# Selective scan: who multiplies the third state of every second group of four

## The reference

```
delta, b, c = split(u @ x_proj_w);  delta = softplus(delta @ dt_proj_w + dt_proj_b)
a = -exp(A_log)
h_t = exp(d_t * a) * h_{t-1} + d_t * b_t * u_t       # for every channel and each of 16 states
y_t = sum over the 16 states of h_t * c_t
y = (y + u * D_param) * silu(x_gate);  out = y @ out_proj_w
```

## Time and profile before

| | us |
|---|---|
| median of 3 runs (lowest, highest) | 2647.35 (2646.22, 2647.95) |
| the profiled execution: its own time | 2645.0 |
| the profiled execution: span of its instructions | 2643.2 |
| the 64 scans: first start, last start | 2329.0, 2521.7 |
| mean granted TensorE clock, share of full speed | 0.984 |

### The profile page before, as it was taken

The page is one execution under the profiler, slowest core; times in us unless marked ns, Lnnn a source line. Parts: engine busy times, 40 slices in busy tenths (PEclk is TensorE's granted clock), DMA queues, the critical chain, the costliest instruction groups (busy, mean ns, idle before and its releaser), DMA issues. The chain is left out here.

```text
span 2643.2 us, 47115 instructions
## 1 busy us (share of the span) xinstructions
PE 2495.8 (94%) x18340; PEld 1932.1 (73%) x18340; DVE 1458.3 (55%) x2420; ACT 1005.5 (38%) x2177; POOL 679.6 (26%) x711
## 2 busy tenths in 40 slices
PE   7889998999999898999999998997999999989999
PEld 4676994666666657967888887894888888467778
DVE  4574225777777743025555556425555555589982
ACT  2252224666666431333222221223222222677731
POOL 2102003001100011013334431203433434057833
PEclk9989998999999999999999999999999999999999
DMA  9353872111110103962212112464121210022210
GB/s 312 123 165 130 299 273 80 45 37 33 33 49 17 54 1 138 327 205 64 72 49 73 61 49 102 153 229 124 61 70 51 73 61 25 27 80 81 86 38 16
DMA packets 98808, 262.25 MB, mean 99 GB/s; under 512 B 19139, under 2 KB 45734, under 8 KB 91062
## 3 DMA queue, kind: packets, MB, share of 16 engines
q1 hardware_dynamic: 86662, 241.84, 27.8%
q0 software_dynamic: 3840, 10.49, 1.3%
q10 hardware_dynamic: 8112, 7.21, 0.8%
HBM read 237.31 MB, written 22.19 MB: 98 GB/s over the span
## 5 line engine op out<-in xcount | busy, mean ns | idle before, releaser
L2685 POOL TENSOR_TENSOR buf<-buf 128x512 f32<-128x512 f32 x128 | 160.0, 1270 | 473.8 <-ACT buf L2831 473.6
L2862 DVE TENSOR_REDUCE buf<-acc 128x256 f32<-128x1024 f32 x128 | 150.8, 1220 | 215.0 <-PE acc L2716 209.8
L2749 PE MATMUL acc<-buf 128*128 128x256 f32 x1024 | 257.0, 384 | 0.0
L2710 PE MATMUL acc<-buf 128*128 128x256 f32 x1024 | 236.6, 384 | 3.2 <-PEq L98 2.3
L2826 ACT COPY buf<-acc 128x256 f32<-128x256 f32 x64 | 23.8, 372 | 532.9 <-PE acc L2731 532.9
L2710 PEld LDWEIGHTS acc<-buf 128*128 128x128 f32 x1024 | 189.4, 190 | 36.6 <-issue 11.8
L2749 PEld LDWEIGHTS acc<-buf 128*128 128x128 f32 x1024 | 180.8, 190 | 33.4 <-issue 15.9
L3227 ACT ACTIVATE buf<-acc,buf 128x512 f32<-128x512 f32 x256 | 172.6, 686 | 75.7 <-DVE buf L3259 75.7
L3259 DVE TENSOR_REDUCE buf<-acc 128x1 f32<-128x512 f32 x256 | 159.0, 684 | 53.6 <-PE acc L3140 53.6
L2875 DVE TENSOR_TENSOR buf<-acc,buf 128x1024 f32<-128x1024 f32 x128 | 150.8, 1220 | 67.8 <-ACT buf L2826 67.8
L3152 PEld LDWEIGHTS acc<-identity,buf 128*128 128x128 f32 x1024 | 114.4, 141 | 82.9 <-issue 78.5
(11 more groups left out here) (506 smaller groups left out, 4768.4 us busy)
## 6 DMA issues: line engine op xcount, KB each, us to landing
buf<-in_L_ffn_W SPq DMA_DIRECT2D x52, 1024.0 KB, 7.0
buf<-in_ctx SPq DMA_DIRECT2D x48, 768.0 KB, 4.5
buf<-in_ctxT SPq DMA_DIRECT2D x64, 512.0 KB, 4.0
buf<-in_L_ffn_w SPq DMA_DIRECT2D x36, 704.0 KB, 5.7
buf<-state_rows SPq DMA_DIRECT2D x32, 512.0 KB, 3.6
buf<-in_ctxT SPq DMA_DIRECT2D x96, 128.0 KB, 4.2
buf<-in_L_ffn_w SPq DMA_DIRECT2D x18, 640.0 KB, 6.4
buf<-in_ctxT SPq DMA_DIRECT2D x32, 256.0 KB, 5.4
```

Source lines behind the costliest of these rows:

```text
L2685: pool.tensor_tensor(quarters[:, 2 * n:2 * n + 2, :], t[:, 4 * n:4 * n + 2, :], t[:, 4 * n + 2:4 * n + 4, :], ALU.add).then_inc(adding, 1)
L2710: pe.matmul(acc_s[:, n, :], ct0[x][:, tile(key_tile(n))], q0[:, b, 4 * y:4 * y + 4, :], start=(n % 2 == 0), stop=False)
L2749: pe.matmul(acc_m[:, 0:ROWS], ctx[x][:, key_tile(n), 0:P], probsT[y][:, n, :], start=(n == 0), stop=(n == KT - 1))
L2862: dve.tensor_reduce(most_of[n][:, :], acc_s[:, 4 * n:4 * n + 4, :].rearrange("p k r -> p r k"), AX.X, ALU.max).then_inc(part_most, 1)
```

## The change

In the quads 1, 3, 5, 7, 9, 11 and 13 (`three_by_pool`), the product R2 goes from DVE to POOL. There POOL's list becomes M0, M1, M2, A0, A1, where M2 multiplies the third state by `crow[1]`; DVE's list becomes s0, s1, s2, s3, R3. The even quads and quad 15 stay as they are. The semaphores count anew: `pool_reads(q)` and `dve_reads(q)` give how many products of each engine lie before quad q. In a changed quad A0 waits for M2 (the instruction just before it on POOL) where it waited for R2. SP's load of `crow[1]` for the quad behind a changed one waits for M2 as well as for R3.

```diff
@@ selective_scan
+            def three_by_pool(q):
+                return q % 2 == 1 and q < QUADS - 1
+
+            def pool_reads(q):
+                return 2 * q + q // 2
+
+            def dve_reads(q):
+                return 2 * q - q // 2
...
                 for m in range(ROUNDS):
+                    before = m // 2 - 1
                     if m >= 2 and m % 2 == 0:
-                        sync.wait_ge(read_by_pool, m)
+                        sync.wait_ge(read_by_pool, pool_reads(before) + 2)
                     elif m >= 2:
-                        sync.wait_ge(read_by_dve, m - 1)
+                        sync.wait_ge(read_by_dve, dve_reads(before + 1))
+                        if three_by_pool(before):
+                            sync.wait_ge(read_by_pool, pool_reads(before) + 3)
...
                 for n in range(UNITS):
                     scan(n)
-                    if n % 4 >= 2:
+                    if n % 4 == 3 or n % 4 == 2 and not three_by_pool(n // 4):
                         read_out(n)
...
                         pool.tensor_tensor(now[:, :], now[:, :], crow[0][:, :], ALU.mult).then_inc(read_by_pool, 1)
+                    if three_by_pool(q):
+                        now = state[(4 * q + 2) % STATES]
+                        pool.wait_ge(rows_in[1], q * 16 + 16)
+                        pool.wait_ge(scanned, 4 * q + 3)
+                        pool.tensor_tensor(now[:, :], now[:, :], crow[1][:, :], ALU.mult).then_inc(read_by_pool, 1)
                     if q < QUADS - 1:
                         for y in range(2):
                             now, other = state[(4 * q + y) % STATES], state[(4 * q + 2 + y) % STATES]
-                            pool.wait_ge(read_by_pool, 2 * q + y + 1)
-                            pool.wait_ge(read_by_dve, 2 * q + y + 1)
+                            pool.wait_ge(read_by_pool, pool_reads(q) + y + 1)
+                            if three_by_pool(q) and y == 0:
+                                pool.wait_ge(read_by_pool, pool_reads(q) + 3)
+                            elif three_by_pool(q):
+                                pool.wait_ge(read_by_dve, dve_reads(q) + 1)
+                            else:
+                                pool.wait_ge(read_by_dve, dve_reads(q) + y + 1)
                             pool.tensor_tensor(now[:, :], now[:, :], other[:, :], ALU.add).then_inc(paired, 1)
```

More of the change, by code:

```diff
@@ L3683, in _ @@
                     if n < UNITS - 2:
-                        pe.wait_ge(read_by_pool, 2 * QUADS - 2 + n % 4 + 1)
+                        pe.wait_ge(read_by_pool, pool_reads(QUADS - 1) + n % 4 + 1)
                     else:
-                        pe.wait_ge(read_by_dve, 2 * QUADS - 2 + n % 4 - 1)
+                        pe.wait_ge(read_by_dve, dve_reads(QUADS - 1) + n % 4 - 1)
                     add_up(n)
```

## The result

The changed kernel takes 2655.32 us (median of 8, 2652.12 to 2659.77) against 2645.72 of the kernel before in the same sessions (median of 8, 2642.35 to 2647.95). The ratio is 1.0035, 95% interval 1.0024 to 1.0046: slower by some 9 us, where 8.7 was forecast. The profiled execution spans 2653.1 us. The 2645.72 is 1.6 under the median of three runs that the prediction was built on (2647.35).

What follows compares the result with a forecast made beforehand. The prediction took one full queue of POOL's and DVE's two-SBUF-input products as the bound. Terms 5.9 + 1.1 + 1.1 + 0.6 for the clock made +8.7, so 2656.1 us; 8-in-10 range 2652.5 to 2659.5.

Steps and rivals of the forecast that it cites:

- What bounds: POOL's products and DVE's two-SBUF-input products exclude each other, forming one full queue of 11.81 us a quad; DVE close second.
- Removing R2: In changed quads, s3 still waits for PE's drive until about 8.1 us; the scan comes forward by 0.1 only.
- Adding M2 and the stretched R3: In changed quads, M2 delays A0, and R3 ends 1.08 behind A0: 13.00 us in place of 11.81, +1.19.
- The wait of A0 for M2: On POOL in a changed quad, A0 waits for the instruction before it: 0.1 us more.
- Quad 9: Despite slack from a PE stall, M2 and A0 stand behind s2 and R3 behind A0 again: +1.1 us.
- Quads 11 and 12: R3 gets in ahead of A0 in quad 11, A0 and A1 slide into quad 12; together about +1.1 us.
- a fall of the clock in quad 12: PE waits about 2.7 us for A0 in quad 12, perhaps then slowing: bounds 0 and 1.4, taken as 0.6.
- The sum: Whole-kernel total: 5.9 for five quads, 1.1, 1.1 and 0.6 for the clock, 8.7 us, giving 2656.1.
- Rival 1: DVE is the bound and gets lighter: changed quads take 10.4 us, -1.4 each, 2637 in all; chance 4%.
- Rival 2: In changed quads R3 goes ahead of A0: +0.6 to +0.8 us each, 2651.6 to 2653; chance 9%.
- Rival 3: No exclusion between M2 or A0 and R3 in changed quads: -1.4 us in all, 2646; chance 2%.
- Rival 4: PE's clock falls in many quads, three to seven more: +4 to +10 us, 2660 to 2666; chance 8%.

Runs made afterwards that it cites:

- e3: Kernel before, with DVE's products R2 and R3 replaced by a maximum with one SBUF input, same waits; ratio 0.997, block 187.99 us.
- e10: Kernel before plus one POOL product of two different tiles into a spare tile in quads 1, 3, ..., 13; 2667.51 us (one run), block 211.42.
- e1: Changed kernel with M2 cut to 8 of 1024 columns, so nobody multiplies the third state; ratio to before 0.9997, block 194.83 us.
- e8: Changed kernel with the gates products of quads 10 and 11 moved to the end of POOL's list; ratio to before 1.0028, block 199.26 us.
- e7: Kernel before with the gates products of quads 10 and 11 moved to the end of POOL's list; ratio 0.9996, block 192.32 us.
- e6: Changed kernel with PE's second add_up of a quad placed behind the drive of s3; ratio to before 1.0045 at most, 1.0033 measured, block 202.33 us.
- e4: Changed kernel with DVE's products replaced by a maximum with one SBUF input, same waits; ratio to before 0.9982, block 191.94 us.
- e9: Kernel before, but in the same seven quads DVE multiplies three states and POOL one; ratio 1.0021, block 201.30 us.
- e11: Kernel before with the same late gates products as e7, run again for a narrower interval; ratio 0.9991, block 192.18 us.
- e2: Kernel before plus one POOL product of a tile with itself into a spare tile in quads 1, 3, ..., 13; ratio 1.0049, block 208.17 us.

## Why the prediction was right

**What bounds.** One queue of POOL's products and DVE's two-input products, full at 11.8, with DVE just behind. Shown from both ends: without the exclusion (e3) all quads but 8 and the last fall to 11.6 and no instruction in the place of R2 or R3 is stretched; with the queue lengthened (e10) they grow by about the length of what was added.

**Removing R2.** Forecast: s3 at 8.1, held by PE. Measured 8.05 (quad 1), idle 1.21 to 1.57. By itself it was worth 0.2 in a quad (e1); the forecast's "0.1 only" for the scan is that.

**Adding M2 and the stretched R3.** Forecast +1.19 a quad, measured +1.24. The wait of A0 for M2 was under-priced: 2.49 to 2.52 from start to start where products without a wait have 2.30 to 2.33, 0.2 and not the 0.1 taken. M2 started 0.04 earlier than worked out, which took half of that back; s3 came slightly earlier than 8.1 and that made no difference, since R3's end hangs on A0. Quad 5 shows how firm that is: s3 there came 0.35 later than in the other quads, R3 was 0.35 shorter (2.33), and the quad took 13.04 all the same.

**Quad 9.** Forecast +1.1, measured -0.16. The term was mis-sized through the clock, not the queue: in the kernel before quad 9 had held a stall behind the fall of the clock in quad 8, and in the changed kernel's profile the clock did not fall there. Where the fall was missing, quad 9 is a plain changed quad, 13.06. The prediction named that possibility and still summed quad 9 at +1.1. So 1.3 us of the block's difference is a fall that one profile has and the other has not, and no run shows what M2 costs in quad 9 with the fall in it.

**Quads 11 and 12.** Forecast +1.1 and, for a fall of the clock in quad 12, 0.6 (half of its price). Measured +2.24: R3 did get in ahead of A0 in quad 11, PE did wait 2.68 (forecast 2.7), and the clock did fall. Removing the backlog (e8) gave 5.1 in the block, where 4.0 belongs to the gates products themselves (e7); the 1.1 between them is the only measure of the wait and the fall together, from one profile each.

**The sum.** 8.04 in the block against 8.7: quad 9 came 1.3 under, quad 12 about 0.5 over, the five plain quads 0.2 over, the rest 0.2 under. The two errors of the clock have opposite signs and partly cancel. The whole time, +9.3 by the ratio, has an interval of 6.4 to 12.2, and 1.9 of the difference between the two profiles lies outside the block. That the time came within 1 us of the forecast 2656.1 is therefore luck; what was understood is the price of a changed quad, 13.03 to 13.06 in place of 11.8, in six quads of the changed kernel and seven of e8.

**The rivals.** Rival 1 fell by e1 and e6. Rival 2 happens if PE's order is changed (e6) and costs what it was said to; with PE's order as it is, it appears in quad 11 only. Rival 3, no exclusion, gets its changed quads of 11.6 only where the exclusion is taken away (e4). Rival 4, a fall in many quads, didn't come: it fell once in the block.

## What to carry to other kernels

Before moving an instruction from a busy engine to an idle one, look for what they share: compare the mean of each instruction with its shortest, and where long ones end a fixed time behind an instruction of the other engine, add both up as one queue. Its price list differs from the engines' own: a product cost 1.08 to 1.23 of the queue on DVE and 2.33 on POOL, so the engine with idle time was the dearer one. Moving a product the other way (e9) cost 1.2 us a quad as well, since DVE had only 0.2 to spare. And ask what else the removed instruction stood in front of: here a third engine came up 1.2 us behind it, and the time it left was filled at once.

## What the runs showed of the hardware

- The exclusion: a DVE product of two SBUF inputs that waits for a POOL product ends 1.07 to 1.09 behind the latter's end (once 1.14, in e6), against a length of 1.23 when free; a maximum with one SBUF input (1.22) and the scan (2.27) never stretch beside POOL.
- When DVE waits and POOL has its next product ready, DVE gets the access at the boundary: in quad 10 of the earlier trace rows, and in all 17 such cases in the blocks of these runs.
- A POOL product of a tile with itself takes 1.89, of two tiles 2.35 (both 128x1024 float32).
- The same wait of PE in quad 8, 2.61 or 2.62, was followed by a clock of 0.50 in the kernel before, e7 and e11 (the `drive` behind it took 3.49 to 3.61), later in the same `drive` in e1 and e2 (2.44 and 2.74), and by no fall in the changed kernel, e3, e4, e8, e9 and e10 (2.02). The row of the changed kernel, to be held against the earlier trace rows:

```profile
2441.25 2.02 PE L3675 MATMUL acc<-buf 128*128 128x128 f32 x16 [2.62 <-DVE buf L3735]
```

What decides it is not shown by these runs; a forecast can only give such a fall a chance.
